# A change to the causal attention prologue: squares of the unrotated heads, cosine products on VectorE, value copies on ScalarE, and a shorter pipeline

## What is computed

```python
def rmsnorm(x, w):
    ms = jnp.mean(x * x, axis=-1, keepdims=True)
    return w * (x * jax.lax.rsqrt(ms + EPS))

def apply_rope(x, cos, sin):
    c = cos[None, :, None, :]
    s = sin[None, :, None, :]
    half = x.shape[-1] // 2
    x1, x2 = (x[..., :half], x[..., half:])
    return jnp.concatenate([x1 * c - x2 * s, x1 * s + x2 * c], axis=-1)

h = rmsnorm(x, ln1_w)
q = (h @ Wq + bq).reshape(batch, seq, NQ, HD)      # NQ = 16 heads of HD = 16
k = (h @ Wk + bk).reshape(batch, seq, NKV, HD)     # NKV = 4
v = (h @ Wv + bv).reshape(batch, seq, NKV, HD)
q = rmsnorm(apply_rope(q, cos, sin), qn_w)
k = rmsnorm(apply_rope(k, cos, sin), kn_w)
...
attn = jax.nn.softmax(causally_masked(scores), axis=-1)
out = jnp.einsum('bhts,bshd->bthd', attn, v)
```

## Time and profile before

| | before |
|---|---|
| median of three runs | 1872.42 us (1869.1 to 1872.81) |
| the profiled execution | 1870.13 us |
| its span, first to last instruction | 1868.3 us |
| mean granted TensorE clock over the span | 0.929 |
| busy: PE, DVE, ACT, POOL | 86%, 59%, 46%, 43% |

### The profile page before, as it was taken

One profiled execution on the slowest core, in us unless ns is written; L12 is line 12 of the kernel. 1 busy time (PEld: TensorE's weight loads), 2 busy tenths in 40 slices (PEclk: granted clock), 3 DMA queues, 4 the chain that ended last, 5 costly groups with the idle time before them and its releaser, 6 DMA issues.

```text
span 1868.3 us, 26191 instructions
## 1 busy us (share of the span) xinstructions
PE 1613.8 (86%) x9225; PEld 1109.1 (59%) x9225; DVE 1096.8 (59%) x2172; ACT 859.4 (46%) x1379; POOL 804.2 (43%) x769
## 2 busy tenths in 40 slices
PE   5953999968976899983996887999999999997988
PEld 3443999955755333363995566555555655563774
DVE  4761465567977355442446598667666777644335
ACT  2422355313336998742452564444454354431463
POOL 3053211213445454423004374666776576745106
PEclk9775999979988899986998998899999999998999
DMA  9613233130000000062112100100010011021454
GB/s 362 241 47 122 81 135 110 53 121 9 1 14 1 1 7 6 7 250 110 48 50 71 49 1 18 58 18 18 18 24 18 7 24 24 1 91 66 134 157 135
DMA packets 68279, 126.41 MB, mean 68 GB/s; under 512 B 9551, under 2 KB 52803, under 8 KB 65464
## 3 DMA queue, kind: packets, MB, share of 16 engines
q1 hardware_dynamic: 60088, 104.56, 16.7%
q0 software_dynamic: 8064, 20.19, 3.3%
HBM read 72.26 MB, written 44.89 MB: 63 GB/s over the span
## 4 chain that ended last, share of the span: by engine, by line
PE 68%; DVE 13%; POOL 6%; issue 5%; DMA 4%; ACT 3%; SPq 0%; POOLq 0%; DVEq 0%; ACTq 0%
PE psum L167 64%; DMA arena<-xb 2%; POOL arena L871 2%; DVE arena L172 1%; DVE arena L1744 1%; POOL xb L1058 1%; POOL arena L1867 1%; DVE arena L188 1%; PE psum L683 1%; DVE arena L1979 1%; ACT arena L1621 1%; DVE arena L1183 1%; PE psum L1370 1%; POOL xb L866 1%; PE psum L207 1%
## 5 line engine op out<-in xcount | busy, mean ns | idle before, releaser
L167 PE MATMUL psum<-arena 128*128 (+15 forms) x5084 | 1019.6, 434 | 96.9 <-DVE arena L1728 16.6
L167 PEld LDWEIGHTS psum<-arena 128*128 128x128 f32 (+4 forms) x5084 | 583.7, 173 | 419.5 <-issue 279.3
L167 PE MATMUL psum<-rounded 128*128 128x256 f32 (+9 forms) x3072 | 525.0, 336 | 10.0 <-DVE rounded L2336 3.5
L167 PEld LDWEIGHTS psum<-rounded 128*128 128x128 f32 (+5 forms) x3072 | 404.0, 184 | 140.6 <-issue 46.0
L2507 POOL TENSOR_TENSOR arena<-arena 128x1024 f32<-128x1024 f32 (+1 forms) x111 | 262.6, 2366 | 88.8 <-ACT arena L2465 80.0
L2416 DVE TENSOR_REDUCE arena<-psum 128x1 f32<-128x512 f32 x256 | 169.5, 681 | 112.4 <-PE psum L167 109.9
L2465 ACT ACTIVATE arena<-psum 128x1024 f32<-128x1024 f32 x144 | 147.2, 1024 | 98.4 <-PE psum L167 97.0
L1621 ACT ACTIVATE arena<-psum,arena 128x1024 f32<-128x1024 f32 x128 | 134.5, 1116 | 21.5 <-PE psum L167 20.3
L871 POOL DMA_INDIRECT arena<-yb,arena x48 | 46.0, 957 | 211.1 <-DMA yb<-arena 197.6
L1211 POOL DMA_INDIRECT yt<-arena x40 | 39.8, 996 | 182.5 <-DVE arena L1174 177.1
L919 DVE SCALAR_TENSOR_TENSOR rounded<-arena,rounded 128x540 fp32r<-128x540 f32 (+1 forms) x96 | 81.8, 885 | 33.4 <-ACT rounded L1120 32.3
(11 more groups left out here) (267 smaller groups left out, 1859.5 us busy)
## 6 DMA issues: line engine op xcount, KB each, us to landing
arena<-in_w SPq DMA_DIRECT2D x8, 2048.0 KB, 8.5
arena<-xb SPq DMA_DIRECT2D x70, 128.0 KB, 2.3
yb<-arena SPq DMA_DIRECT2D x70, 128.0 KB, 1.7
arena<-in_w1u SPq DMA_DIRECT2D x4, 2048.0 KB, 14.5
rounded<-rounded SPq DMA_DIRECT2D x64, 128.0 KB, 2.2
xb<-arena SPq DMA_DIRECT2D x3, 2048.0 KB, 16.0
xb<-arena SPq DMA_DIRECT2D x2, 2064.0 KB, 31.6
arena<-xb SPq DMA_DIRECT2D x8, 516.0 KB
```

The lines of the kernel that those rows point to most:

```text
L167: return e.matmul(o, l, r, start=start, stop=stop, skip_group_check=True)
```

## The change

- The squares are taken of `QKV` (unrotated) and not of RO, so ACT can square as soon as QKV is there.
- The cosine product moves from POOL to DVE, beside the sine product. The value copy moves from POOL to ACT. POOL keeps only the two products L1849 and L1850.
- In each step DVE now does QKV of a tile, the low parts of the tile three back, both products, the reciprocals of the tile one back, the rotation, and the sum of squares of the same tile.
- PE does the ten transposes ahead of the product of the same step, and they are those of the tile five back. The turns of the input are packed into the first four steps (`TURNS1`).
- ACT does roots, squares, value copy, high parts and, last in a step, the kept copies. The loops of PE and ACT have NT + 5 steps, and that of DVE ends with step NT + 3, where all three had NT + 7.

```diff
         f1_XGT, f1_XG = view(o + 15360, 2, 2, 128), view(o + 15872, 2, 256)
         f1_Y, f1_G = view(o + 14848, 2, 256), view(o, 8, 256)
         s_f1w, s_f1c, s_vx, s_rs2 = sem("f1_w_in"), sem("f1_consts"), sem("v_blank"), sem("rstd2")
-        s_pj, s_qkv, s_t1, s_ri = sem("qkv_prod"), sem("qkv_ready"), sem("cos_part_and_v"), sem("head_rstd")
+        s_pj, s_qkv, s_vxc, s_ri = sem("qkv_prod"), sem("qkv_ready"), sem("v_kept"), sem("head_rstd")
         s_ro, s_sq, s_ms, s_rh = sem("roped"), sem("squares"), sem("mean_sq"), sem("roots")
         s_qn, s_h, s_l = sem("head_normed"), sem("qk_high"), sem("qk_low")
         s_tr, s_ka, s_kd = sem("qk_turned"), sem("q_kept"), sem("k_kept")
...
                                          sem("block_y"))
 
 
+        TURNS1 = {0: (2,), 1: (3, 4), 2: (5, 6), 3: (7,)}
         PACKED = (2, 3, 6, 7, 10, 11)
 
         ORDER = (("w8", "w9", "w10"), ("w11", "t0"),
...
             for i in range(2):
                 pe_turn(e, 3, i, (s_xn, 48 + 2 * i + 2))
             e.wait_ge(s_f1c, 2)
-            for t in range(NT + 7):
-                if t < 6:
-                    pe_turn(e, 3, t + 2, (s_xn, 48 + 2 * t + 6))
+            for t in range(NT + 5):
+                if 0 <= t - 5 < NT:
+                    pe_qk_turn(e, t - 5)
+                for i in TURNS1.get(t, ()):
+                    pe_turn(e, 3, i, (s_xn, 48 + 2 * i + 2))
                 if t < NT:
                     e.wait_ge(s_xt, 24 + t // 2 + 1)
                     if t >= 2:
...
                     for k in range(2):
                         m = mm(e, psum[:, t % 2, 0:384], XT[:, k, 128 * t:128 * t + 128], WQ[:, k, :], k == 0, k == 1)
                     m.then_inc(s_pj, 1)
-                if 0 <= t - 7 < NT:
-                    pe_qk_turn(e, t - 7)
             e.wait_ge(s_ka, NT)
             e.wait_ge(s_kd, NT)
-            e.wait_ge(s_t1, NT)
+            e.wait_ge(s_vxc, NT)
             e.wait_ge(s_qkv, NT)
             for u in range(len(UNITS) + 8):
                 if u < len(UNITS):
...
             e.wait_ge(s_rs2, 1)
             e.activation(RS2, VE, ACT.Sqrt).then_inc(s_rh, 1)
             e.wait_ge(s_vx, 2)
-            for i in range(NT + 7):
-                if i < 6:
-                    act_turn(e, 3, i + 2)
-                t = i - 7
+            for i in range(NT + 5):
+                for x in TURNS1.get(i, ()):
+                    act_turn(e, 3, x)
+                t = i - 2
                 if 0 <= t < NT:
-                    e.wait_ge(s_tr, t + 1)
-                    e.activation(QT[:, :, 128 * t:128 * t + 128], turned1(t)[2], ACT.Copy).then_inc(s_ka, 1)
-                    e.activation(KT[:, :, 128 * t:128 * t + 128], turned1(t)[3], ACT.Copy).then_inc(s_kd, 1)
-                t = i - 5
+                    e.wait_ge(s_ms, t + 1)
+                    e.activation(RSH[:, t % 4, :], MSH[:, t % 4, :], ACT.Sqrt, bias=EPS, scale=1.0 / 16).then_inc(s_rh, 1)
+                    if t == NT - 1:
+                        act_table(e, ACT.Exp)
+                t = i - 1
+                if 0 <= t < NT:
+                    e.wait_ge(s_qkv, t + 1)
+                    if t >= 5:
+                        e.wait_ge(s_ms, t - 4)
+                    e.activation(SQ[:, t % 5, :], QKV[:, t % 2, 0:320], ACT.Square).then_inc(s_sq, 1)
+                    e.activation(VX[:, t, :, 0:16], QKV[:, t % 2, 320:384].rearrange("p (v c) -> p v c", v=4),
+                                 ACT.Copy).then_inc(s_vxc, 1)
+                t = i - 3
                 if 0 <= t < NT:
                     r3, qq, kk = parts1(t)
                     e.wait_ge(s_qn, t + 1)
...
                         e.wait_ge(s_tr, t - 2)
                     e.activation(qq[:, :, 0:3:2, :], bc(r3[:, 0:16, :], 2, 2), ACT.Copy)
                     e.activation(kk[:, :, 0:2, :], bc(r3[:, 16:20, :], 2, 2), ACT.Copy).then_inc(s_h, 1)
-                t = i - 3
+                t = i - 5
                 if 0 <= t < NT:
-                    e.wait_ge(s_ms, t + 1)
-                    e.activation(RSH[:, t % 4, :], MSH[:, t % 4, :], ACT.Sqrt, bias=EPS, scale=1.0 / 16).then_inc(s_rh, 1)
-                    if t == NT - 1:
-                        act_table(e, ACT.Exp)
-                t = i - 2
-                if 0 <= t < NT:
-                    e.wait_ge(s_ro, t + 1)
-                    if t >= 5:
-                        e.wait_ge(s_ms, t - 4)
-                    e.activation(SQ[:, t % 5, :], RO[:, t % 4, :], ACT.Square).then_inc(s_sq, 1)
+                    e.wait_ge(s_tr, t + 1)
+                    e.activation(QT[:, :, 128 * t:128 * t + 128], turned1(t)[2], ACT.Copy).then_inc(s_ka, 1)
+                    e.activation(KT[:, :, 128 * t:128 * t + 128], turned1(t)[3], ACT.Copy).then_inc(s_kd, 1)
             e.wait_ge(s_tr, NT)
             e.wait_ge(s_l, NT)
             for u in range(len(UNITS) + 8):
...
             m.then_inc(s_f1c, 1)
             e.wait_ge(s_rh, 1)
             settle(e, dve, e.reciprocal(RS2, RS2))
-            t2 = {}
-            for i in range(NT + 7):
-                t = i - 3
-                if 0 <= t < NT:
-                    e.wait_ge(s_sq, t + 1)
-                    e.tensor_reduce(MSH[:, t % 4, :], SQ[:, t % 5, :].rearrange("p (h c) -> p h c", c=16), AX.X,
-                                    ALU.add).then_inc(s_ms, 1)
-                t = i - 6
+            for i in range(1, NT + 4):
+                t = i - 1
+                if t < NT:
+                    e.wait_ge(s_pj, t + 1)
+                    if t >= 2:
+                        e.wait_ge(s_vxc, t - 1)
+                    e.scalar_tensor_tensor(out=QKV[:, t % 2, :], in0=psum[:, t % 2, 0:384], scalar=RS2[:, t:t + 1],
+                                           in1=sml("bqkv"), op0=ALU.mult, op1=ALU.add).then_inc(s_qkv, 1)
+                t = i - 4
                 if 0 <= t < NT:
                     r3, qq, kk = parts1(t)
                     e.wait_ge(s_h, t + 1)
                     e.scalar_tensor_tensor(qq[:, :, 1, :], r3[:, 0:16, :], 1.0, qq[:, :, 0, :], ALU.mult, ALU.subtract)
                     e.scalar_tensor_tensor(kk[:, :, 2, :], r3[:, 16:20, :], 1.0, kk[:, :, 0, :], ALU.mult, ALU.subtract).then_inc(s_l, 1)
-                t = i - 4
+                t = i - 1
+                if t < NT:
+                    e.wait_ge(s_qkv, t + 1)
+                    for tab, T_ in ((cst("cos"), T1), (cst("sin"), T2)):
+                        m = e.tensor_tensor(T_[:, t % 2, :].rearrange("p (h c) -> p h c", c=8),
+                                            QKV[:, t % 2, 0:320].rearrange("p (h c) -> p h c", c=8),
+                                            bc(tab.rearrange("p (t c) -> p t c", c=8)[:, t % 8, :], 1, 40), ALU.mult)
+                    dve.n += 1
+                    m.then_inc(dve.sem, 1)
+                t = i - 2
                 if 0 <= t < NT:
                     e.wait_ge(s_rh, t + 2)
                     e.reciprocal(RSH[:, t % 4, :], RSH[:, t % 4, :]).then_inc(s_ri, 1)
-                t = i - 2
-                if 0 <= t < NT:
+                t = i - 1
+                if t < NT:
                     r4 = RO[:, t % 4, :].rearrange("p (h a c) -> p h a c", a=2, c=8)
                     a4 = T1[:, t % 2, :].rearrange("p (h a c) -> p h a c", a=2, c=8)
                     b4 = T2[:, t % 2, :].rearrange("p (h a c) -> p h a c", a=2, c=8)
-                    e.wait_ge(s_t1, t + 1)
-                    e.wait_ge(dve.sem, t2[t])
+                    e.wait_ge(dve.sem, dve.n)
                     if t >= 4:
                         e.wait_ge(s_l, t - 3)
                     e.tensor_tensor(r4[:, :, 0, :], a4[:, :, 0, :], b4[:, :, 1, :], ALU.subtract)
                     e.tensor_tensor(r4[:, :, 1, :], a4[:, :, 1, :], b4[:, :, 0, :], ALU.add).then_inc(s_ro, 1)
-                t = i - 1
-                if 0 <= t < NT:
-                    s = t % 2
-                    e.wait_ge(s_pj, t + 1)
-                    if t >= 2:
-                        e.wait_ge(s_t1, t - 1)
-                    e.scalar_tensor_tensor(out=QKV[:, s, :], in0=psum[:, t % 2, 0:384], scalar=RS2[:, t:t + 1],
-                                           in1=sml("bqkv"), op0=ALU.mult, op1=ALU.add).then_inc(s_qkv, 1)
-                    e.wait_ge(s_qkv, t + 1)
-                    sn = cst("sin").rearrange("p (t c) -> p t c", c=8)[:, t % 8, :]
-                    dve.n += 1
-                    e.tensor_tensor(T2[:, s, :].rearrange("p (h c) -> p h c", c=8),
-                                    QKV[:, s, 0:320].rearrange("p (h c) -> p h c", c=8), bc(sn, 1, 40),
-                                    ALU.mult).then_inc(dve.sem, 1)
-                    t2[t] = dve.n
+                    e.wait_ge(s_sq, t + 1)
+                    e.tensor_reduce(MSH[:, t % 4, :], SQ[:, t % 5, :].rearrange("p (h c) -> p h c", c=16), AX.X,
+                                    ALU.add).then_inc(s_ms, 1)
             for u in range(len(UNITS) + 8):
```

(24 more changed lines are left out.)

## The result

The changed kernel takes 1845.88 us (median of four runs, 1845.13 to 1848.68) against 1872.2 (1869.1 to 1872.81): a ratio of 0.9865, with a 95% interval of 0.9848 to 0.9883. The profiled execution took 1846.27 with a span of 1843.7, 24.6 less than before.

A forecast was written before the change was run, and what follows sets the result against it. It took a ring through PE, ACT and DVE, 4.0 us per tile, to bind; afterwards DVE's queue, 3.44. Last QKV 9.8 us earlier plus 4.2 at the end made 14.0 off, 1858 us; range 1851 to 1866.

The forecast's parts named there:

- The ring over two tiles: Prologue before the change: a chain of dependences through PE, ACT and DVE takes 8.0 us for two tiles, 4.0 per tile.
- What lay above 4.0: Prologue before: the trace's 4.34 per tile exceeds 4.0 because some groups, such as transposes of 2.34 us, ran at lower clock.
- DVE's queue: Prologue after the change: DVE's own instructions set the pace, 3.44 us per tile, bounds 2.95 and 3.9.
- The blocking of the second half of the rotation stays: DVE's step: POOL's product still holds off that instruction, so it takes 0.85 where its twin takes 0.33.
- rival (b): DVE's step: the rotation meets no POOL product, 3.44 falls to 2.95, 6 us more gain, 1852; chance 0.07.
- The lower bound of 2.95: DVE's step if the rotation meets no POOL product: 0.78 becomes about 0.27.
- The rest of DVE's sum: DVE's step: the pitches of low parts, both products, QKV, reciprocals and sum of squares, added towards 3.44 us.
- The value copy: taken at 0.2: ACT's step: this added copy of 64 columns costs 0.2 us, making ACT's sum 2.66, under 3.44.
- the cover of 0.4 to 0.8: ACT's step: slack per tile between ACT's sum of 2.66, at most 3.06, and DVE's 3.44 us.
- The beginning: First steps up to the fourth QKV: 0.9 us lost, bounds 0 and 2, fourth QKV at 551.1.
- The end: Last QKV to first score: 11.7 us where it was 15.9, 4.2 gained through the shorter pipeline.
- Rival (a) and (e): Prologue, PE at lower clock: for a third to half the tiles, 1861 to 1865, chance 0.13; throughout, 1877, chance 0.05.

The follow-up runs named there:

- experiments 4, 5 and 6: Kernel before, one edit each: squares of unrotated heads alone, 1870.7 us; kept copies last on ACT alone, 1859.61; rotation ahead of the reciprocals on DVE, 1866.1.
- experiment 3: Changed kernel with a second cosine product on DVE, into an unused place: 1855.55 us, pace 3.21 per tile.
- experiment 10: Changed kernel with the cosine product back on POOL, the value copy staying on ACT: 1854.15 us, pace 3.13 per tile.
- experiment 1: Changed kernel without the wait for the rotation ahead of POOL's normalising product: 1855.92 us, nearly all steps 3.36 to 3.39.
- experiment 12: Changed kernel with ACT's table load behind the high parts of tile 15 instead of behind its roots: 1847.95 us.
- experiment 9: Changed kernel with transposes and kept copies seven steps back, as in the kernel before: 1861.12 us.

## Why the prediction was wrong

- **What bounds the kernel before: right.** The ring over two tiles is shown by experiments 4, 5 and 6: an edit outside it does nothing, opening it gives DVE's 3.61 to a hundredth, and making the rotation 0.53 cheaper takes 0.44 off two steps at the full clock (8.12 to 7.68). What lay above 4.0 was rightly put down to the lower clock: the long pairs of steps are those with transposes of 2 us and more.
- **What is left after: right in kind, wrong in size.** DVE's queue sets the pace one for one (experiment 3). The step that failed is the sentence "The blocking of the second half of the rotation stays: POOL's product L1849 is released by the reciprocals as before". The forecast had 0.78 for that pitch and 0.24 for the first half; they are 0.23 (574.82 to 575.05) and 0.17. That is 0.62 of the 0.63 between 3.44 and 2.81, and 12 x 0.63 = 7.6 us is the whole excess of the middle. "Released as before" was true of what releases it and false of when: POOL's product got a second wait and starts 0.41 after the reciprocals and not 0.35; the rotation lost one wait and starts its second half 0.36 to 0.37 after them and not 0.45. A race that POOL won by 0.10 is now lost by 0.05. Both waits are in the diff, and both starts were in the earlier trace rows, 0.10 apart; a margin that small should have been named as a race, with the two outcomes as near equals. The table in experiment 10 shows that POOL's second wait turned it. It stood instead as rival (b), 1852, with a chance of 0.07, and for it "speaks only that POOL has less in its queue". With the block in place, as in experiment 1, the stretch from first QKV to first score is 59.8 us, where the forecast had 604.1 - 541.8 = 62.3, and the total 1855.9, near the 1858 that was forecast. The other 0.07 of the 0.62, the pitch of the first half, has no cause that is shown. The lower bound of 2.95 that the prediction gave the step was too high for the same reason: it had 0.27 for the freed second half and left the first at 0.24.
- **The rest of DVE's sum: right.** Low parts 0.35 and 0.14 for 0.33 and 0.13, both products 0.80 for 0.82, QKV 0.53 for 0.54, reciprocals 0.19 for 0.21, sum 0.40 for 0.39.
- **The value copy: taken at 0.2, and it costs 0.14 to 0.15** of ACT's queue (its duration is 0.24). ACT was covered, but barely: at a step of 2.81 hardly any of the cover of 0.4 to 0.8 was left. ACT was busy for 29.9 of the 32 us from 552 to 584, and stood for 0.1 between roots and squares (581.60 to 581.70). The calculation of that cover leaned on the step of 3.44.
- **The beginning: -0.9 forecast, +0.45 measured.** The sign was wrong, again because the rotation isn't blocked, and because it no longer waits for POOL's cosine product (0.36): the third step took 2.45 where it was 3.24. The ACT copies that I feared did hold QKV up in the first step (2.83 for 2.58, of which 0.29 are DVE's wait for the squares), though experiment 12, with the same beginning, has 2.56 there. The forecast was for the time of the fourth QKV, 551.1; it came at 550.20, after a first QKV that was 0.5 late, with nothing edited ahead of it.
- **The end: 4.2 forecast, 3.3 measured.** The last 20 transposes ran at the lower clock, 4.20 us (590.77), so that the last two kept copies waited for PE by 0.65 and 0.54; I had them wait for nothing.
- **Rival (a) and (e), the clock:** neither came. The granted clock was 1.00 from 544 to 584 us and 0.50 from 588 to 592, after PE had waited 1.49 and 1.22 us for DVE's low parts with only transposes left to do (585.00 and 587.54). The transposes that began at 587.54 took 2.27.
- **What was carried on unchanged:** the first score to the end gave 2.9 us where nothing was forecast, and the medians another 1.7 beyond the spans. Nothing behind the first score was edited, and over the kernels that stretch spreads by 8 us without relation to the edits, so I take both for variation between executions; that isn't shown by itself. The stage alone gives 22 us, which is still 8 more than forecast.
- **A step that was right by luck:** the prediction put the shorter pipeline down to the end alone. Experiment 9 shows that with the old lag the new order of ACT makes a ring of 3.5 us per tile; that the change had the shorter lag too was not reckoned with.

## What to carry to other kernels

Write a stall in a software pipeline down as a ring, with the number of tiles over which it closes: the same 8 us of work cost 4.0 per tile over two tiles (8.12 for two at the full clock) and would cost 2.7 over three, so that DVE's 3.61 bound instead; moving two instructions within one queue decided which it was. Where a two-input VectorE instruction and a GpSimd one start within a tenth of a microsecond of each other, the order of the starts is a result of its own, here worth half a microsecond per step; look at the waits ahead of each, and forecast both outcomes. After such a change, measure what the old slack is now: ACT's and PE's cover of 0.8 us was computed for a step that turned out 0.6 shorter.

## What the runs showed that I had not expected

One wait more ahead of POOL's product, for something long done, moved its start by 0.07 us: 0.41 after the reciprocals with two waits and 0.34 with one (experiment 1). By itself that is nothing; as the referee of a race it was worth 0.56 us per step and 5.6 us of the stage (the medians are 10 apart). And the block strikes both ways: the POOL product that lost took 0.85 to 0.92 in place of 0.73.
